# Gate products of a GRU in f16 passes, one sum moved to GpSimd, and a different split of the adjacency count

## Chip, cores and metric

The kernel runs on one core of a Trainium2 chip. The metric is the device time of one launch in microseconds (us). Before the change it was 1576.88 us, the median of three runs (1576.55 to 1579.28).

## What is computed

x has 8192 rows (nodes) of 128 features, adj is 8192 x 8192. Two residual layers, each after a layer norm and a ReLU:

```
h   = relu(layernorm(x))
Wh  = h @ W;  e = leaky_relu(Wh@a[:128] + (Wh@a[128:]).T, 0.2)
att = softmax(where(adj > 0, e, -9e15));  h' = att @ Wh
gi  = h' @ w_ih.T + b_ih;  gh = h @ w_hh.T + b_hh
r = sigmoid(gi_r + gh_r); z = sigmoid(gi_z + gh_z); n = tanh(gi_n + r * gh_n)
x   = x + (1 - z) * n + z * h
x   = x + adj @ (relu(layernorm(x)) @ W1.T + b1)
```

## The kernel before

The main path assumes that adj holds only zeros and ones, and finds out by counting whether that is so. A register read of `redo` at the end decides whether a second, general path (`any_adjacency`) is run; with the given inputs it isn't.

**Preparation.** x is loaded and normalised, transposed and multiplied with W. GpSimd (POOL) scales the gate weights by 64 (L401, L402), makes an f16 high and low part of w_ih (L404, L406, tile `wihT`), and an f16 unit matrix (L408). w_hh stays f32 (`whhT`).

**Layer 1.** 32 row blocks of 256 rows. A block is worked through in 4 chunks (c = 0 to 3) of 16 column tiles each. For each chunk SP loads 2 MB of adj into X (two buffers, L315), the Vector engine (DVE) makes mask bytes Y (`ones_of`, L662), SP stores Y to DRAM for layer 2 (L311), DVE and the Scalar engine (ACT) compare scores (L713, L491: 6 and 10 tiles of 16), DVE combines them to two masks (L721, L725), and TensorE (PE) multiplies the masks with the table TB in f16 (L970, 258 columns, 64 matmuls for each chunk and mask half). ACT counts the nonzero elements in the first SEEN = 7/8 of each chunk of X (`count`, L501); block 0 isn't counted here. When both readers are done with a buffer (c_y, c_cnt), SP loads the next chunk into it.

The GRU of a block is threaded into the slots of later blocks; PE's part stands in `after`. `attended` (L983) transposes h', `gates` (L997 to L1001) makes the gate sums of two halves t: a bias matmul of 512 columns, three f16 matmuls of 384 columns with w_ih (high times high, high times low, low times high), and two f32 matmuls with w_hh of 256 and 128 columns, on h transposed (HT, f32). ACT then takes the sigmoids (`gate_sigmoids`, L517) and the tanh (`candidate`, L522, tile nn). DVE does `gated` (L730, L732) in chunk 1 and `rows_step` in chunk 2: h - n (L744), times z (L753), x + n (L762), the sum of both (L768), then statistics. POOL adds EPS and takes the power -1/2 (L414, L417). SP stores x after the update and loads x, h and HT of a block (`rows_load`, L300 to L304). ACT copies PE's sums out of PSUM (`evacuate`, L511), and PE waits for that before it writes them for the next block.

**Layer 2.** For each row block t, PE multiplies the stored mask bytes with the projected features (L1055), DVE adds the halves of the mask (`halved`, L847), ACT sums them (`ones_sum`, L577), and DVE finishes the rows (`finish`, L863, L868). In between ACT loads and counts what layer 1 left out (`late_load`, `late_count`, L581 to L593): the 4 chunks of block 0 whole, then the last eighths of 8 chunks at a time, 20 loads in all. After the last halves `tally` (L889 to L893) compares the two counts; `sums` (L1088, L1090) stands in PE's queue in the middle of the last row block; `judge` and the last matmul (L1109) give the verdict, and SP waits for the last stores (L363) before all engines read `redo` and branch.

Each engine has its own queue, in the order of the code above; the order of the pieces within a slot is written out by hand, and semaphores join the queues.

Of the kernel before, what the change touches and what calls it, by code (L numbers as in the profile page):

```python
# [6 lines left out]
F = 128  # L7
P = 128
# [18 lines left out]
RW = 256  # L27
NS = N // RW
JC = 16
CS = NT // JC  # L30
# [3 lines left out]
MARK = 0.5  # L34
# [7 lines left out]
SEEN = JC * RW * 7 // 8  # L42
COUNTED = (NS - 1) * CS
LATE = CS + NS // 2
# [13 lines left out]
def graph_layers(nc, xb, adj, adjb, w, wt, a, w_ih, w_hh, wiht, whht, b_ih, b_hh, w1, w1t, b1, out):  # L58
    outer = ExitStack()
    with outer:  # L60
        def sem(name):
            return outer.enter_context(nc.semaphore(name))

        redo = outer.enter_context(nc.sbuf_tensor("redo", [1, 1], mybir.dt.int32))
        binary_adjacency(nc, sem, redo, xb, adjb, w, wt, a, wiht, whht, b_ih, b_hh, w1t, b1, out)
# [5 lines left out]
def binary_adjacency(nc, sem, redo, xb, adjb, w, wt, a, wiht, whht, b_ih, b_hh, w1t, b1, out):  # L71
    ctx = ExitStack()
    with ctx:
# [24 lines left out]
        wihT = sb("wihT", [P, 2, 3 * F], f16)  # L98
        whhT = sb("whhT", [P, 3 * F])
# [20 lines left out]
        nz = sb("nz", [P, NS // 2, 2 * CS + 1])  # L120
        cy = sb("cy", [P, NS])
        odd = sb("odd", [P, NS // 2, 2])
# [30 lines left out]
        wihf = rzf[:, P:P + 3 * F]  # L153
# [8 lines left out]
        bhid = TBf[0:2, 2 * F:4 * F].bitcast(f32)  # L162
# [36 lines left out]
        d_hi = t_lo  # L199
        q_half = t_p  # L200
# [19 lines left out]
        q_out = [sem(f"q_out{b}") for b in range(2)]  # L220
# [30 lines left out]
        with nc.Block() as block:  # L251
            @block.sync
            def _(sp):
                for q in range(8):
                    sp.dma_start(H[:, q * 8:(q + 1) * 8, :], xb[:, q * 8:(q + 1) * 8, :]).then_inc(p_x[q], 16)
                for dst, src in ((brow[0:3, :], b_ih.rearrange("(r c) -> r c", c=F)),
                                 (bhid, b_hh[0:2 * F].rearrange("(r c) -> r c", c=F)),
# [4 lines left out]
                for k in range(16):  # L262
# [8 lines left out]
                    if k == 9:  # L271
                        sp.wait_ge(p_bias, 7)
# [4 lines left out]
                sp.wait_ge(b_in, 112)  # L277
# [45 lines left out]

                each_row_block(sp, slot, 1)
# [37 lines left out]
                for u in range(2):  # L362
                    sp.wait_ge(q_out[u], NS // 2 * 16)  # L363

            @block.gpsimd
            def _(pool):
# [4 lines left out]
                nc.gpsimd.memset(onesb[:, :], 1.0)  # L371
                nc.gpsimd.memset(BI[:, :], 0.0).then_inc(p_one, 1)
                pool.wait_ge(p_id, 1)
# [13 lines left out]
                pool.wait_ge(b_in, 64)  # L387
                nc.gpsimd.tensor_tensor(brow[0:2, :], brow[0:2, :], bhid, ALU.add).then_inc(p_bias, 1)
                pool.wait_ge(p_bias, 1)
                nc.gpsimd.tensor_scalar(brow[0:4, :], brow[0:4, :], WSCALE, None, ALU.mult).then_inc(p_bias, 1)  # L390
                src = [brow] + bres
                for k in range(3):
                    pool.wait_ge(p_bias, 2 * k + 2)
                    nc.gpsimd.tensor_copy(bpart[k], src[k]).then_inc(p_bias, 1)
                    if k < 2:
                        pool.wait_ge(p_bias, 2 * k + 3)
# [3 lines left out]
                pool.wait_ge(wt_in, 48)  # L400
# [23 lines left out]
            def _(act):  # L424
# [4 lines left out]
                act.dma_start(wihf, wiht).then_inc(wt_in, 16)  # L429
                act.dma_start(whhT[:, :], whht).then_inc(wt_in, 16)  # L430
# [39 lines left out]
                def table_high(i):  # L470
                    act.wait_ge(t_p, i + 1)
                    if i == 0:
                        act.wait_ge(b_in, 112)
# [40 lines left out]
                def gate_sigmoids(q):  # L514
                    act.wait_ge(g_b, q + 1)
                    wait(act, d_x1, q)
                    nc.scalar.activation(rz[:, :, :], GP3[:, :, 0:2 * F], ACT.Sigmoid,  # L517
# [61 lines left out]
                def late_load(n):  # L579
                    if n < CS:  # L580
                        act.dma_start(Z[n % 2], adjb[n, :, :]).then_inc(c_in[n % 2], 16)  # L581
                    else:
                        first, last = max((n - CS) * 2 * CS, CS), (n - CS + 1) * 2 * CS
# [24 lines left out]
            def _(dve):  # L608
# [118 lines left out]
                def gated(q):  # L727
                    dve.wait_ge(g_2, q + 1)
                    wait(dve, g_3, q)
                    nc.vector.tensor_tensor(tmp[:, :, :], rz[:, :, 0:F], GP3[:, :, 3 * F:4 * F], ALU.mult).then_inc(d_rh, 1)  # L730
                    dve.wait_ge(d_rh, q + 1)
                    nc.vector.tensor_tensor(tmp[:, :, :], tmp[:, :, :], GP3[:, :, 2 * F:3 * F], ALU.add).then_inc(d_tmp, 1)  # L732

                def rows_step(qa, q, u, n):
# [3 lines left out]
                    xtv = XT[u].rearrange("p (t f) -> p t f", f=F)  # L738
# [12 lines left out]
                    if updating:  # L751
                        dve.wait_ge(d_u, q * 3 + 1)
# [8 lines left out]
                    if updating:  # L761
                        nc.vector.tensor_tensor(xtv, xtv, nn[:, :, :], ALU.add).then_inc(d_u, 1)  # L762
# [3 lines left out]
                    if updating:  # L766
                        dve.wait_ge(d_u, q * 3 + 3)
# [40 lines left out]
                def slot(g, u, k):  # L808
                    main = in_range(g, 0)
                    first = isinstance(g, int) and g == 0  # L810
                    for c in range(CS):
# [16 lines left out]
                        if c == 1 and in_range(g, 2):  # L828
                            gated(g - 2)
# [41 lines left out]
                def examine():  # L871
# [10 lines left out]
                    nc.vector.tensor_tensor(rzf[:, 0:3 * F], wihT[:, 0, :], wihT[:, 0, :], ALU.mult).then_inc(k_v, 1)  # L882
# [887 lines left out]
```

## Time and profile before

| | us |
|---|---|
| median of 3 runs | 1576.88 |
| the profiled execution | 1577.86 |
| its span, first to last instruction | 1576.0 |
| PE busy | 1508.2 (96%) |
| DVE busy | 1364.9 (87%) |
| ACT busy | 1350.7 (86%) |
| POOL busy | 135.3 (9%) |
| mean granted clock of TensorE | 0.985 |

Busy time counts instructions that work, not waits. Shares over the whole span mix the stages; layer 1 lies between about 62 and 1122 us, layer 2 behind it. In the rows below, L is the line in the kernel before, `out<-in` the tiles that an instruction writes and reads, and `<-` in brackets what ended an idle time.

### The profile page before, as it was taken

How to read it: one execution, taken by the hardware profiler on the slowest of the kernel's cores; microseconds unless marked ns; L12 is line 12 of the kernel's file. 1: busy time of each engine (PE TensorE's matmuls, PEld its weight loads, DVE VectorE, ACT ScalarE, POOL GpSimd, SP SyncE). 2: the span in 40 equal slices, each digit the busy share in tenths (PEclk: the TensorE clock that was granted, in tenths of full speed). 3: DMA queues.
4: the chain of work that ended last, by engine and by line, in shares of the span. 5: the costliest groups of instructions: out<-in, count | busy, mean ns of one | idle time of the engine just before them, and what ended most of it. 6: DMA issues, size and time to landing. Idle time of an engine off the chain costs nothing.

```text
span 1576.0 us, 35430 instructions
## 1 busy us (share of the span) xinstructions
PE 1508.2 (96%) x13356; PEld 1333.0 (85%) x13388; DVE 1364.9 (87%) x2161; ACT 1350.7 (86%) x1952; POOL 135.3 (9%) x96
## 2 busy tenths in 40 slices
PE   5468999999999999999999999999999999999997
PEld 4357888888888888888888888888888888888887
DVE  8898999999999999999999999997479977666684
ACT  5789999999999999999999999997175898875463
POOL 5100010001000110011000100010000000000000
PEclk9788999999999999999999999999999999999999
DMA  8859999999999999999999999997276999864430
GB/s 311 296 214 362 346 351 355 348 343 348 358 350 349 341 356 346 353 335 355 347 350 340 358 349 350 343 349 286 116 312 237 401 374 363 320 256 163 178 128 16
DMA packets 96085, 486.68 MB, mean 309 GB/s; under 512 B 9432, under 2 KB 38690, under 8 KB 75042
## 3 DMA queue, kind: packets, MB, share of 16 engines
q1 hardware_dynamic: 78322, 444.54, 75.4%
q10 hardware_dynamic: 17712, 41.49, 6.9%
q8 instruction: 28, 0.46, 0.1%
q14 instruction: 23, 0.19, 0.0%
HBM read 402.07 MB, written 83.92 MB: 308 GB/s over the span
## 4 chain that ended last, share of the span: by engine, by line
PE 93%; DVE 4%; ACT 1%; DMA 1%; issue 1%; DVEq 0%; ACTq 0%
PE ACC L970 56%; PE ACC L1055 28%; PE GP L999 2%; PE GP L1000 2%; PE GQ L1018 1%; ACT M L491 1%; PE GP L1001 1%; DVE TB L703 1%; DVE JK L612 1%; DVE AE L698 1%; DVE JK L698 1%; DMA h_columns<-AE 1%; DVE M L629 0%; PE TG L983 0%; PE TG L1007 0%
## 5 line engine op out<-in xcount | busy, mean ns | idle before, releaser
L970 PE MATMUL ACC<-TB,M 128*128 128x258 f16 x8192 | 928.1, 275 | 38.1 <-DVE M L721 31.0
L970 PEld LDWEIGHTS ACC<-TB,M 128*128 128x128 fp8e4 x8192 | 805.0, 98 | 143.6 <-issue 39.3
L491 ACT ACTIVATE M<-SB,dsteep 128x256 fp8e4<-128x256 f32 x1304 | 533.9, 504 | 0.0
L501 ACT ACTIVATE JK<-X 128x3584 uint8<-128x3584 uint32 x124 | 395.1, 3186 | 0.0
L662 DVE TENSOR_SCALAR Y<-X 128x4096 fp8e4<-128x4096 f32 x128 | 292.2, 2283 | 28.9 <-DMA X<-in_adjb_dram 28.4
L577 ACT ACTIVATE TB<-TB 128x8192 uint8<-128x8192 fp8e4 x32 | 225.0, 7030 | 102.8 <-DVE TB L847 90.6
L1055 PE MATMUL ACC<-WG,X 128*128 128x256 f16 x2048 | 225.5, 273 | 0.0
L1055 PE MATMUL ACC<-WG,TB 128*128 128x256 f16 x2048 | 225.4, 273 | 0.0
L1055 PEld LDWEIGHTS ACC<-WG,TB 128*128 128x128 fp8e4 x2048 | 200.4, 98 | 23.2
L1055 PEld LDWEIGHTS ACC<-WG,X 128*128 128x128 fp8e4 x2048 | 200.3, 98 | 23.1
L713 DVE TENSOR_SCALAR M<-SB,nd 128x256 fp8e4<-128x256 f32 x744 | 205.6, 346 | 0.0
L721 DVE TENSOR_TENSOR M<-M,Y 128x1024 uint32<-128x1024 uint32 x128 | 156.1, 1219 | 19.8 <-ACT M L491 18.6
L725 DVE TENSOR_TENSOR M<-Y,M 128x1024 uint32<-128x1024 uint32 x128 | 156.8, 1225 | 4.4
L414 POOL TENSOR_TENSOR ve<-mv,epst 128x2 f32<-128x2 f32 x32 | 63.0, 1969 | 985.7 <-DVE mv L792 985.7
L847 DVE TENSOR_TENSOR TB<-X 128x8192 fp8e4<-128x8192 fp8e4 x16 | 138.9, 8685 | 4.4 <-ACT TB L577 3.5
L847 DVE TENSOR_TENSOR TB<-TB 128x8192 fp8e4<-128x8192 fp8e4 x16 | 138.9, 8681 | 1.7 <-ACT TB L577 1.7
L863 DVE SCALAR_TENSOR_TENSOR hp<-ACC,R 128x256 f32<-128x256 f32 x32 | 13.5, 423 | 96.0 <-PE ACC L1055 94.2
L593 ACT ACTIVATE JK<-M 128x4096 uint8<-128x4096 uint32 (+1 forms) x20 | 70.3, 3516 | 2.6 <-DMA M<-in_adjb_dram 2.6
L417 POOL TENSOR_TENSOR rstd<-ve,half 128x2 f32<-128x2 f32 x32 | 48.0, 1501 | 2.5
L999 PE MATMUL GP<-wihT,hpT 128*128 128x384 f16 x192 | 41.7, 326 | 1.7
L511 ACT ACTIVATE AE<-ACC 128x516 f32<-128x516 f32 x64 | 37.7, 589 | 5.8 <-PE ACC L970 5.8
L1000 PE MATMUL GP<-whhT,R 128*128 128x256 f32 x128 | 38.1, 379 | 0.0
(142 smaller groups left out, 784.8 us busy)
## 6 DMA issues: line engine op xcount, KB each, us to landing
X<-in_adjb_dram SPq DMA_DIRECT2D x128, 2048.0 KB, 9.7
mask_bytes<-Y SPq DMA_DIRECT2D x128, 512.0 KB, 5.9
M<-in_adjb_dram ACTq DMA_DIRECT2D x19, 2048.0 KB, 11.7
X<-mask_bytes SPq DMA_DIRECT2D x16, 2048.0 KB, 9.3
TB<-mask_bytes SPq DMA_DIRECT2D x16, 2048.0 KB, 9.0
M<-in_xb_dram SPq DMA_DIRECT2D x8, 512.0 KB, 8.3
h_rows<-M SPq DMA_DIRECT2D x8, 512.0 KB, 4.2
R<-in_xb_dram SPq DMA_DIRECT2D x32, 128.0 KB, 6.7
```

Of the source, the lines that this page charges most:

```text
L491: ins = nc.scalar.activation(rows(mask1(c), jj), SB[u][:, :], ACT.Sigmoid, scale=STEEP, bias=dsteep[:, j:j + 1], saturate=False)
L501: nc.scalar.activation(junk[:, 0:SEEN], X[c % 2][:, 0:SEEN].bitcast(u32), ACT.Sign, accum_out=nz[:, bass.ds(k, 1), at:at + 1].rearrange("p ...
L577: nc.scalar.activation(junk8, halves[t % 2], ACT.Copy, accum_out=cy[:, t:t + 1]).then_inc(q_sum, 1)
L593: nc.scalar.activation(junk[:, 0:cols], Z[n % 2][:, 0:cols].bitcast(u32), ACT.Sign, accum_out=nz[:, k:k + 1, at:at + 1].rearrange("p k c - ...
L662: nc.vector.tensor_scalar(Y[c % 2][:, :].bitcast(f8), X[c % 2][:, :], 1.0, MARK, ALU.is_equal, ALU.mult, saturate=False).then_inc(c_y, 1)
L713: ins = nc.vector.tensor_scalar(rows(mask1(c), jj), SB[u][:, :], nd[:, j:j + 1], None, ALU.is_ge, saturate=False)
L721: nc.vector.tensor_tensor(mask1(c), mask1(c), Y[c % 2][:, :], ALU.bitwise_and).then_inc(c_m1, 1)
L725: nc.vector.tensor_tensor(mask2(c), Y[c % 2][:, :], mask1(c), ALU.bitwise_xor).then_inc(c_m2, 1)
L847: nc.vector.tensor_tensor(halves[b % 2], YB[b][:, 0:N], YB[b][:, N:2 * N], ALU.add, saturate=False).then_inc(q_half, 1)
L970: ins = nc.tensor.matmul(A[t][m][:, 0:2 * TW], rows((mask1, mask2)[m](c), jj)[:, t * P:(t + 1) * P], TB[:, c * JC + jj, m, 0:2 * TW], star ...
L999: nc.tensor.matmul(bank[:, 0:3 * F], left, wihT[:, part, :], start=False, stop=False)
L1055: ins = nc.tensor.matmul(PH2[b][:, d * 2 * F:(d + 1) * 2 * F], YB[b][:, j * RW + d * P:j * RW + (d + 1) * P], GS[:, j, :], start=(d == 0 a ...
```

## The change

- **Gates.** w_hh gets f16 high and low parts like w_ih; one tile `GW` holds both (columns n, r, z of w_ih and r, z, n of w_hh). h transposed gets them too (`HH`): DVE makes them in chunk 1 of a slot, between the two operations of `gated`. PE makes three f16 matmuls of 384 columns with them in place of the two f32 ones; PE now waits for the low part (d_hl) and no longer for the load of HT. The order of the gate columns in PSUM is n, r, z, h_n.
- **Sum.** x + n leaves DVE's `rows_step` and goes to POOL, ahead of L414 in its slot; DVE waits for it (d_xn) before L768.
- **Count.** SEEN is 13/16 in place of 7/8, so layer 2 counts 3/16 of a chunk, 5 chunks in a load: 29 loads in place of 20. The tally adds up to one number in place of 16.
- **Weights and biases.** Both gate matrices are loaded into R by three DMAs in place of two and prepared in three POOL operations on 768 columns. SP waits for them (p_bias 12) before its first slot, and for a memset of POOL before the bias loads, of which there are 5 in place of 4.
- **End.** The wait for the last stores stands behind the branch on `redo`, on SP.

```diff
-SEEN = JC * RW * 7 // 8
+SEEN = JC * RW * 13 // 16
+GROUP = 5
-LATE = CS + NS // 2
+LATE = CS + 25
...
         with nc.If(needed != 0):
+            for eng in (nc.sync, nc.scalar, nc.vector, nc.tensor, nc.gpsimd):
+                for u in range(2):
+                    eng.wait_ge(q_out[u], NS // 2 * 16)
             any_adjacency(nc, outer, xb, adj, w, a, w_ih, w_hh, b_ih, b_hh, w1, b1, out)
+        for u in range(2):
+            nc.sync.wait_ge(q_out[u], NS // 2 * 16)
...
+                sp.wait_ge(p_bias, 12)
                 each_row_block(sp, slot, 1)
...
-                for u in range(2):
-                    sp.wait_ge(q_out[u], NS // 2 * 16)
...
-                nc.gpsimd.tensor_scalar(wihf, wihf, WSCALE, None, ALU.mult).then_inc(p_bias, 1)
-                nc.gpsimd.tensor_scalar(whhT[:, :], whhT[:, :], WSCALE, None, ALU.mult).then_inc(p_bias, 1)
-                pool.wait_ge(p_bias, 8)
-                nc.gpsimd.tensor_copy(wihT[:, 0, :], wihf).then_inc(p_bias, 1)
+                nc.gpsimd.tensor_scalar(wraw, wraw, WSCALE, None, ALU.mult).then_inc(p_bias, 1)
+                pool.wait_ge(p_bias, 9)
+                nc.gpsimd.tensor_copy(GW[:, 0, :, :], wrawv).then_inc(p_bias, 1)
                 pool.wait_ge(p_bias, 10)
-                nc.gpsimd.tensor_tensor(wihT[:, 1, :], wihf, wihT[:, 0, :], ALU.subtract).then_inc(p_bias, 1)
+                nc.gpsimd.tensor_tensor(GW[:, 1, :, :], wrawv, GW[:, 0, :, :], ALU.subtract).then_inc(p_bias, 1)
...
                     if in_range(g, 2):
                         q = g - 2
+                        xtv = XT[u].rearrange("p (t f) -> p t f", f=F)
+                        pool.wait_ge(g_3, q + 1)
+                        pool.wait_ge(g_in[u], k * 48)
+                        nc.gpsimd.tensor_tensor(xtv, xtv, nn[:, :, :], ALU.add).then_inc(d_xn, 1)
                         pool.wait_ge(d_mv, q + 1)
...
-                    k, at = (0, n) if n < CS else (n - CS, 2 * CS)
-                    cols = JC * RW // 2 if n == CS else JC * RW
+                    k, at = (0, n) if n < CS else ((n - CS) % 16, 2 * CS + (n - CS) // 16)
+                    parts = min(GROUP, NS * CS - CS - (n - CS) * GROUP)
+                    cols = JC * RW if n < CS else parts * (JC * RW - SEEN)
...
+                def gate_step(qh, u, n, q):
+                    halving, gating = qh is not None, q is not None
+                    if halving:
+                        dve.wait_ge(g_in[u], (n + 1) * 48)
+                        wait(dve, g_b, qh)
+                        dve.sem_inc(turn, 1)
+                        nc.vector.tensor_copy(HH[:, 0, :], HT[u]).then_inc(d_hh, 1)
+                    if gating:
...
+                    if halving:
+                        dve.wait_ge(d_hh, qh + 1)
+                        nc.vector.tensor_tensor(HH[:, 1, :], HT[u], HH[:, 0, :], ALU.subtract).then_inc(d_hl, 1)
...
-                    if updating:
-                        nc.vector.tensor_tensor(xtv, xtv, nn[:, :, :], ALU.add).then_inc(d_u, 1)
...
                     if updating:
-                        dve.wait_ge(d_u, q * 3 + 3)
+                        dve.wait_ge(d_u, q * 2 + 2)
+                        dve.wait_ge(d_xn, 16 + q + 1)
                         nc.vector.tensor_tensor(x1, x1, XT[u], ALU.add).then_inc(d_x1, 1)
...
-                    pe.wait_ge(g_in[u], (n + 1) * 48)
+                    pe.wait_ge(d_hl, q + 1)
...
                         for left, part in ((a_t, 0), (a_t, 1), (a_l, 0)):
-                            nc.tensor.matmul(bank[:, 0:3 * F], left, wihT[:, part, :], start=False, stop=False)
-                        nc.tensor.matmul(bank[:, 0:2 * F], h_t, whhT[:, 0:2 * F], start=False, stop=False)
-                        ins = nc.tensor.matmul(bank[:, 3 * F:4 * F], h_t, whhT[:, 2 * F:3 * F], start=False, stop=True)
+                            nc.tensor.matmul(bank[:, 0:3 * F], left, GW[:, part, 0, :], start=False, stop=False)
+                        for left, part in ((h_t, 0), (h_t, 1), (h_l, 0)):
+                            ins = nc.tensor.matmul(bank[:, F:4 * F], left, GW[:, part, 1, :], start=False,
+                                                   stop=(left is h_l))
```

## Rows read from the trace of the kernel before

**Rows 1.** The page, chain of work that ended last, shares by engine.
```profile
PE 93%; DVE 4%; ACT 1%; DMA 1%; issue 1%; DVEq 0%; ACTq 0%
```

**Rows 2.** Busy time by stretch: PE, PEld, DVE, ACT, POOL, PEclk, DMA share, GB/s.
```profile
340.49:660.27 319.78, 319.25 (x2832) 282.00 (x2841) 304.14 (x571) 315.28 (x550) 37.06 (x20) 1.00 0.93 348
...
1152.00:1560.50 408.50, 408.50 (x3745) 366.17 (x3743) 304.33 (x105) 298.74 (x105) 0.00 (x0) 1.00 0.69 264
```

**Rows 3.** The same chain in order of time: start, length.
```profile
115.38 7.16 issue
122.53 16.77 PE ACC L970 x128
...
596.31 7.04 PE ACC L970 x64
...
628.29 7.04 PE ACC L970 x64
```

**Rows 4.** Waits between 340.49 and 660.27: total, times, longest.
```profile
DVE Y L662 <- DMA X<-in_adjb_dram: 8.0, 14, 1.2
DVE M L721 <- ACT M L491: 5.8, 10, 0.8
ACT rz L517 <- PE GP L1001: 4.5, 10, 0.5
```

**Rows 5.** Timeline of PE, end of one gate group: start, length.
```profile
626.99 0.65 PE L999 MATMUL GP<-wihT,hpT 128*128 128x384 f16 x3
627.48 0.59 PE L1000 MATMUL GP<-whhT,R 128*128 128x256 f32 x2
627.91 0.38 PE L1001 MATMUL GP<-whhT,R 128*128 128x128 f32 x2
628.13 7.20 PE L970 MATMUL ACC<-TB,M 128*128 128x258 f16 x64
```

**Rows 6.** Groups by line and shape, whole run: busy, mean ns, idle before.
```profile
L501 ACT ACTIVATE JK<-X 128x3584 uint8<-128x3584 uint32 x124 | 395.1, 3186 | 0.0
...
L593 ACT ACTIVATE JK<-M 128x4096 uint8<-128x4096 uint32 x19 | 68.4, 3602 | 2.6 <-DMA M<-in_adjb_dram 2.6
...
L762 DVE TENSOR_TENSOR R<-R,nn 128x256 f32<-128x256 f32 x32 | 13.3, 417 | 0.0
...
L684 DVE COPY tmp<-GP 64x128 f32<-64x128 f32 x1 | 0.3, 276 | 0.0
...
L406 POOL TENSOR_TENSOR wihT<-rz,wihT 128x384 f16<-128x384 f32 x1 | 0.9, 919 | 0.1
```

**Rows 7.** Timeline of ACT where PE first waits for it.
```profile
121.85 0.58 ACT L511 ACTIVATE AE<-ACC 128x516 f32<-128x516 f32 x1
```

**Rows 8.** Timeline of DVE and POOL around one small POOL sum.
```profile
612.65 2.26 DVE L662 TENSOR_SCALAR Y<-X 128x4096 fp8e4<-128x4096 f32 x1
...
612.82 2.15 POOL L414 TENSOR_TENSOR ve<-mv,epst 128x2 f32<-128x2 f32 x1 [28.20 <-DVE mv L792]
```

**Rows 9.** All 32 of that POOL sum: min/median/max ns.
```profile
L414 POOL TENSOR_TENSOR ve<-mv,epst x32: 196/2152/2154, 165.9 to 1141.9; 128x2 f32<-128x2 f32 x32
```

**Rows 10.** Timeline of one update of x: candidate, and its last sum.
```profile
605.23 0.41 ACT L522 ACTIVATE nn<-tmp 128x256 f32<-128x256 f32 x1
...
609.28 0.42 DVE L768 TENSOR_TENSOR R<-R 128x256 f32<-128x256 f32 x1
```

**Rows 11.** Timeline at the start, POOL's last preparation and DVE's resumption.
```profile
43.33 0.29 POOL L408 CAST identh<-ident 128x128 f16<-128x128 f32 x1
...
45.82 0.26 DVE L669 TENSOR_REDUCE bad<-WG 128x1 f32<-128x64 f32 x1 [3.79 <-ACT WG L440]
```

**Rows 12.** Timeline near the end: DVE's tally and PE's use.
```profile
1556.35 0.30 DVE L889 TENSOR_REDUCE odd<-nz 128x16 f32<-128x144 f32 x1 [1.88 <-ACT TB L577]
...
1560.37 0.29 PE L1088 MATMUL GP<-odd,ones 128*128 128x16 f32 x2
```

**Rows 13.** Waits of SP's queue at the end.
```profile
SPq L363 <- DMA out_dram<-R: 1.3, 1, 1.3
```

More of the change, by code:

```diff
@@ L64, in graph_layers, with binary_adjacency @@
         redo = outer.enter_context(nc.sbuf_tensor("redo", [1, 1], mybir.dt.int32))
-        binary_adjacency(nc, sem, redo, xb, adjb, w, wt, a, wiht, whht, b_ih, b_hh, w1t, b1, out)
+        q_out = [sem(f"q_out{b}") for b in range(2)]
+        binary_adjacency(nc, sem, q_out, redo, xb, adjb, w, wt, a, wiht, whht, b_ih, b_hh, w1t, b1, out)
         needed = nc.values_load(redo[0:1, 0:1], min_val=0, max_val=1)
         with nc.If(needed != 0):
+            for eng in (nc.sync, nc.scalar, nc.vector, nc.tensor, nc.gpsimd):
+                for u in range(2):
+                    eng.wait_ge(q_out[u], NS // 2 * 16)
             any_adjacency(nc, outer, xb, adj, w, a, w_ih, w_hh, b_ih, b_hh, w1, b1, out)
-def binary_adjacency(nc, sem, redo, xb, adjb, w, wt, a, wiht, whht, b_ih, b_hh, w1t, b1, out):
+        for u in range(2):
+            nc.sync.wait_ge(q_out[u], NS // 2 * 16)
+def binary_adjacency(nc, sem, q_out, redo, xb, adjb, w, wt, a, wiht, whht, b_ih, b_hh, w1t, b1, out):
     ctx = ExitStack()
@@ L97, in binary_adjacency @@
         h2T = sb("h2T", [P, RW])
-        wihT = sb("wihT", [P, 2, 3 * F], f16)
-        whhT = sb("whhT", [P, 3 * F])
+        GW = sb("GW", [P, 2, 2, 3 * F], f16)
+        HH = sb("HH", [P, 2, RW], f16)
         w1T = sb("w1T", [P, F])
@@ L161, in binary_adjacency @@
         brow = TBf[0:5, 0:2 * F].bitcast(f32)
-        bhid = TBf[0:2, 2 * F:4 * F].bitcast(f32)
+        bhid = TBf[0:5, 2 * F:4 * F].bitcast(f32)
         bres = [TBf[0:5, (4 + 2 * k) * F:(6 + 2 * k) * F].bitcast(f32) for k in range(2)]
@@ L199, in binary_adjacency @@
         d_hi = t_lo
+        d_hh, d_hl = sem("d_hh"), sem("d_hl")
+        d_xn = p_hd
         q_half = t_p
@@ L255, in _ @@
                     sp.dma_start(H[:, q * 8:(q + 1) * 8, :], xb[:, q * 8:(q + 1) * 8, :]).then_inc(p_x[q], 16)
-                for dst, src in ((brow[0:3, :], b_ih.rearrange("(r c) -> r c", c=F)),
-                                 (bhid, b_hh[0:2 * F].rearrange("(r c) -> r c", c=F)),
+                sp.wait_ge(p_bias, 1)
+                for dst, src in ((brow[0:1, :], b_ih[2 * F:3 * F].rearrange("(r c) -> r c", c=F)),
+                                 (brow[1:3, :], b_ih[0:2 * F].rearrange("(r c) -> r c", c=F)),
+                                 (bhid[1:3, :], b_hh[0:2 * F].rearrange("(r c) -> r c", c=F)),
                                  (brow[3:4, :], b_hh[2 * F:3 * F].rearrange("(r c) -> r c", c=F)),
@@ L386, in _ @@
                     deviation(q)
-                pool.wait_ge(b_in, 64)
-                nc.gpsimd.tensor_tensor(brow[0:2, :], brow[0:2, :], bhid, ALU.add).then_inc(p_bias, 1)
-                pool.wait_ge(p_bias, 1)
+                pool.wait_ge(b_in, 80)
+                nc.gpsimd.tensor_tensor(brow, brow, bhid, ALU.add).then_inc(p_bias, 1)
+                pool.wait_ge(p_bias, 2)
                 nc.gpsimd.tensor_scalar(brow[0:4, :], brow[0:4, :], WSCALE, None, ALU.mult).then_inc(p_bias, 1)
@@ L516, in gate_sigmoids @@
                     wait(act, d_x1, q)
-                    nc.scalar.activation(rz[:, :, :], GP3[:, :, 0:2 * F], ACT.Sigmoid,
+                    nc.scalar.activation(rz[:, :, :], GP3[:, :, F:3 * F], ACT.Sigmoid,
                                          scale=1.0 / WSCALE).then_inc(g_2, 1)
@@ L582, in late_load @@
                     else:
-                        first, last = max((n - CS) * 2 * CS, CS), (n - CS + 1) * 2 * CS
+                        first = CS + (n - CS) * GROUP
+                        last = min(first + GROUP, NS * CS)
                         act.dma_start(Z[n % 2][:, 0:(last - first) * (JC * RW - SEEN)].rearrange(
@@ L725, in combine @@
                     nc.vector.tensor_tensor(mask2(c), Y[c % 2][:, :], mask1(c), ALU.bitwise_xor).then_inc(c_m2, 1)
[L727 to L732, printed above, removed]
+                def gate_step(qh, u, n, q):
[6 more added lines that the diff above has]
+                    if gating:
+                        dve.wait_ge(g_2, q + 1)
+                        wait(dve, g_3, q)
+                        nc.vector.tensor_tensor(tmp[:, :, :], rz[:, :, 0:F], GP3[:, :, 3 * F:4 * F], ALU.mult).then_inc(
+                            d_rh, 1)
+                    if halving:
+                        dve.wait_ge(d_hh, qh + 1)
+                        nc.vector.tensor_tensor(HH[:, 1, :], HT[u], HH[:, 0, :], ALU.subtract).then_inc(d_hl, 1)
+                    if gating:
+                        dve.wait_ge(d_rh, q + 1)
+                        nc.vector.tensor_tensor(tmp[:, :, :], tmp[:, :, :], GP3[:, :, 0:F], ALU.add).then_inc(d_tmp, 1)
                 def rows_step(qa, q, u, n):
@@ L827, in slot @@
                             combine(g, c)
-                        if c == 1 and in_range(g, 2):
-                            gated(g - 2)
+                        if c == 1:
+                            gate_step(g - 1 if in_range(g, 1) else None, 1 - u, k if u else k - 1,
+                                      g - 2 if in_range(g, 2) else None)
                         if c == 2:
@@ L1087, in sums @@
                     pe.wait_ge(k_df, 4)
-                    nc.tensor.matmul(GP[:, 0:NS // 2], ones[:, :], odd[:, :, 0:1].rearrange("p g o -> p (g o)"), start=True,
-                                     stop=True)
+                    nc.tensor.matmul(GP[:, 0:1], ones[:, :], odd[:, 0:1], start=True, stop=True)
                     nc.tensor.matmul(GP[:, P:2 * P], ones[:, :], tmp[:, 0, :], start=True, stop=True).then_inc(k_w, 1)
```

49 lines of the change are left out of this document (26 added, 23 removed).

## The prediction

> **What bounds the kernel now.** I read three views in this order. First the chain of work that ended last: 93% of it is TensorE (PE) [rows 1]. Then the same chain in time: PE resumes at 122.53 us and from there the pieces join without a hole until layer 2 ends; the 64 products of one chunk return at 596.31 and 628.29 us, so one row block takes 31.98 us [rows 3]. Then ten such periods in one window of 319.78 us: PE busy 319.25, the Scalar engine (ACT) 315.28, the Vector engine (DVE) 304.14, the DMA engines 93% [rows 2]. Four resources stand within 7% of each other, so each must be asked what it can give. ACT's only idle time in the ten periods is 4.5 us, all of it waiting for PE's gate sums, thus 0.45 us for a block; DVE's waits are 8.0 us on loads of X and 5.8 us on ACT's masks [rows 4], in all 15.6 us idle (319.78 - 304.14), 1.56 us for a block. PE waits for nobody. So layer 1 is PE's, with ACT 0.45 us behind it. In layer 2 PE is busy 408.50 of 408.50 us, while ACT has 298.74 and DVE 304.33 [rows 2].
>
> **PE's part.** For each half t of a block the change takes out the two f32 matmuls on w_hh and puts three f16 ones of 384 columns in. Start to start in the trace: three f16 matmuls of 384 columns take 627.48 - 626.99 = 0.49 us, the f32 one of 256 columns 627.91 - 627.48 = 0.43, the f32 one of 128 columns 628.13 - 627.91 = 0.22 [rows 5]. Out go 0.65 us, in come 0.49: -0.16 us, -0.32 for the two halves. All 32 gate groups lie in PE's unbroken stretch, the last two of them between products of layer 2, so the term is 32 x 0.32 = **-10.2 us**. The new block takes 31.66 us, if the others keep up.
>
> **ACT's part.** A count of 4096 takes 3602 ns, of 3584 3186 ns [rows 6], 0.81 ns an element; 256 elements fewer are -0.21 us, four times a block -0.83. ACT's work falls from 31.53 (31.98 - 0.45) to 30.7 us, below 31.66: this makes room, and is no gain by itself in the steady part. It is one at the start. PE stands idle for 7.16 us from 115.38 [rows 3], until ACT has copied out the sums of block 0 at 121.85 + 0.58 [rows 7]. Ahead of that copy stand three counts of block 1's chunks in ACT's queue, so PE resumes 3 x 0.21 = **-0.6 us** earlier.
>
> **DVE's part.** DVE loses x + n, 417 ns, and gets the subtraction for the low part, which is an operation of that shape: 417 ns [rows 6]. The copy that makes the high part (256 f32 to f16) is not in the trace. The nearest rows are a copy of 64x128, 276 ns, below, and the 417 ns above; I take 280, because the row is a copy too. The subtraction fills the gap that `gated` leaves between its two operations, which I count as nothing. So DVE's work becomes 30.41 + 0.28 = 30.7 us. PE's gates wait for both new operations; DVE makes them just behind the sigmoids of the previous group, so most of a block of 31.98 us ahead of PE's next group. The copy itself waits for the load of HT, issued by SP in the slot before, and for PE's last gate group, for which the sigmoids beside it wait anyway: nothing. Behind it queue `gated` and the compares of the next chunk; PE, which takes their masks, waits for none in the ten periods [rows 4].
>
> **POOL's part.** The moved sum starts when nn is there, 605.23 + 0.41 = 605.64 us, and L768 needs it at 609.28 less the 0.33 that x + n took of DVE's queue: 3.3 us [rows 10]. The sum of 384 columns takes 919 ns, the same engine's sum of 2 columns 196 ns when nothing else runs [rows 6, 9]; in proportion 256 columns are an estimated 0.68 us. But the sum of 2 columns has a median of 2152 ns, and at 612.82 it ended only when DVE's L662 did, 612.65 + 2.26 = 614.91 [rows 8, 9]: POOL waits for some DVE instructions. The instruction running at 605.64 is at most 1.2 us long, so the sum should be ready by about 607.5. The opposite may happen too, that DVE waits for POOL; between nothing and the 919 ns I take the whole 0.68 us of the sum as lost to DVE. That gives 30.7 + 0.68 = 31.4 us for DVE, still under 31.66, by 0.3 us. The cover is thin here, and the rivals start from it.
>
> The Trainium skill, SBUF — State Buffer, "Who interferes with whom", states that a DVE instruction with two SBUF inputs and a GpSimd instruction that reads SBUF exclude each other for a whole instruction, whichever issues first. By that rule DVE pays the sum's time each block, which is the value in my sum; a reading of the rows alone would allow nothing, and DVE 30.7 us.
>
> **DMA.** Layer 1 moves the same bytes in 1% less time: from 93% to about 94%. X loads are issued when ACT's count is done, which now comes 0.2 us earlier, so I expect no new wait.
>
> **Layer 2.** ACT gets 9 more loads to count. Before: 19 of 3602 ns and one of half; after: 4 of 3602, 24 of about 3.4 us, one of 2.8: 99 in place of 70 us, and 9 accumulator reads. ACT comes to about 330 of 408 us. At the end of the layer, where the counts now reach up to the last two sums, the tally may come some 0.4 us later; it is at 1556.35, and PE asks for it at 1560.37 [rows 12], so PE hides it. Extra DMA traffic of 16 MB finds engines that are at 69% [rows 2]. Zero.
>
> **Start.** POOL's three operations on 768 columns in place of 384 add some 2 us to work that ended at 43.62, and DVE resumes on its own chain at 45.82 [rows 11]: hidden, with a bound of +0.5 us where POOL runs into it. SP's new wait for it comes later still. The additional small loads are issued long before their users. Zero.
>
> **End.** SP waits 1.3 us for the last stores [rows 13] before the engines meet and read `redo`. Moved behind the branch, this wait runs beside that reading: **-1.3 us** (bounds: 0 and -1.7, if the meeting costs something too).
>
> **Sum.** -10.2 - 0.6 - 1.3 = -12.1 us. The profiled execution took 1577.86 us (span 1576.0 and 1.86 around it), so it would take 1565.8. The median of the runs lies 0.98 lower: **1564.8 us**.
>
> **Rivals.**
> - *DVE becomes the bound by a little.* With the upper bounds, the copy 0.417 and POOL's hold 0.919, and the 0.18 us of idle time a block that no wait explains (1.56 - 0.80 - 0.58), DVE needs 30.41 + 0.42 + 0.92 + 0.18 = 31.9 us. Then layer 1 gives only some 0.05 x 30 = 1.5 us in place of 9.6; the time is 1564.8 + 8.1 = 1573, and between the bounds it is about 1569. For it: 31.4 is near 31.66. Against it: part of DVE's waits were for ACT and loads and vanish when it is late. Chance 0.11.
> - *POOL and DVE block each other for long (slower).* The place is the moved sum, among DVE's instructions with two inputs. If DVE stands still for as long as the small POOL sum lasts in the trace, 2.15 us, it needs 30.41 + 0.28 + 2.15 + 0.18 = 33.0 us, and 30 blocks cost 30 x 1.04 = +31 us, less 1.9: about 1606. It decides from a hold of 1.1 us, where DVE passes 31.98. Against it: those 2.15 us are POOL's waiting for DVE, since it ended 0.06 us after L662 [rows 8]. Chance 0.07.
> - *The DMA engines hold the pace.* At 93% busy, with DVE waiting for X in 14 of 40 chunks [rows 4], loads may already set the period. Then PE's gain turns into waits for masks, and only -1.9 is left: 1575. Against it: PE never waits, and X lands up to 1.2 us late only because it is issued as late as ACT lets it. Chance 0.05.
> - *The forecast.* Chance 0.77.
>
> **From these to the numbers.** A change of 0.2%, 3.15 us, is about what a measurement of this kernel can tell from none. Faster: the forecast and nearly all of the first rival, 0.86; within: 0.07, the DMA rival and the end of the first; slower: 0.07. The range: below, the end's bound (-0.4), more than three counts' worth at the start, and the spread of the runs give 1561; above, the first rival gives 1573. What lies outside is the slower rival and the DMA one, 0.12, and some of the runs' spread.
>
> **What would show it.** Right: the products of a chunk return every 31.66 us; one gate half takes 1.19 us, with six f16 matmuls; ACT's wait for the gates is longer than 0.45 us, near 0.9; PE has no wait for masks after about 122 us; PE's first wait ends 0.6 us earlier; DVE busy goes up by 0.2 to 0.3 us a block, and L725 or L744 is longer or late once a block. Wrong: a period above 31.7 us, PE waiting for DVE's L721 or L725 in the steady part, L768 waiting for POOL, layer 2 longer than 408.5 us for the same products, or the time after the last store unchanged.

## The result and the profile after

| | before | after |
|---|---|---|
| median of 4 runs, us | 1576.72 | 1563.76 |
| range | 1575.62 to 1579.28 | 1563.26 to 1563.96 |
| span of the profiled execution | 1576.0 | 1562.2 |

The ratio is 0.9915, 95% interval 0.9898 to 0.9932: 13.0 us less, where 12.1 were predicted (1564.8 us, range 1561 to 1573).

First the page of the changed kernel: who is on the chain that ended last, and how busy each engine is.

```profile
PE 1498.8 (96%) x13324; PEld 1310.0 (84%) x13324; DVE 1386.4 (89%) x2193; ACT 1354.8 (87%) x1970; POOL 168.3 (11%) x129
...
PE 93%; DVE 5%; ACT 1%; issue 1%; DMA 0%; POOL 0%; DVEq 0%; ACTq 0%
```

TensorE still holds 93% [rows 1]. Its busy time fell by 9.4 us, while that of the Vector engine rose by 21.5 and that of GpSimd by 33.0 (1386.4 and 168.3, from 1364.9 and 135.3).

Ten row blocks of the steady part, and layer 2, in the view by stretch (columns as in [rows 2]: length, PE, PEld, DVE, ACT, POOL, clock, DMA share, GB/s):

```profile
281.09:597.57 316.48, 316.48 (x2822) 274.74 (x2821) 310.44 (x581) 307.54 (x552) 45.17 (x30) 1.00 0.94 353
...
1139.97:1548.47 408.50, 408.50 (x3746) 366.06 (x3743) 305.30 (x105) 326.84 (x123) 0.00 (x0) 1.00 0.80 304
```

Ten blocks take 316.48 us, 31.65 each, in place of 31.98. The Scalar engine fell from 315.28 to 307.54 us for ten blocks; the Vector engine rose from 304.14 in a longer window to 310.44 in a shorter one: 31.04 us of 31.65, 98%. Layer 2's long stretch takes 408.50 us as before, with the Scalar engine at 326.84 (298.74 before) and DMA at 80% (69% before).

The same ten blocks, who waited for whom; it answers to [rows 4]:

```profile
ACT rz L533 <- PE GP L1031: 8.9, 10, 0.9
DVE Y L680 <- DMA X<-in_adjb_dram: 2.1, 5, 0.7
DVE M L739 <- ACT M L507: 1.1, 3, 0.4
```

TensorE is not in the list, so it still waits for nobody. The Scalar engine's wait for the gates doubled to 0.89 us a block: the room that the shorter counts made lies idle. The Vector engine's waits fell from 13.8 us to 3.2.

One gate half in the timeline of TensorE (start, length); it answers to [rows 5]:

```profile
588.51 0.38 PE L1027 MATMUL GP<-BI,onesb 128*128 128x512 bf16 x1
588.73 0.65 PE L1029 MATMUL GP<-GW,hpT 128*128 128x384 f16 x3
589.22 0.65 PE L1031 MATMUL GP<-GW,HH 128*128 128x384 f16 x3
589.70 7.20 PE L1000 MATMUL ACC<-TB,M 128*128 128x258 f16 x64
```

Six f16 matmuls of 384 columns stand where three f16 and two f32 stood. From 588.73 to 589.22 and on to 589.70 it is 0.49 and 0.48 us; the second was 0.65. The whole half takes 1.19 us (588.51 to 589.70).

The update of x in the timeline, with GpSimd's sum:

```profile
598.65 0.41 ACT L538 ACTIVATE nn<-tmp 128x256 f32<-128x256 f32 x1
...
599.22 0.73 POOL L427 TENSOR_TENSOR R<-R,nn 128x256 f32<-128x256 f32 x1 [20.48 <-ACT nn L538]
599.30 1.74 DVE L743 TENSOR_TENSOR M<-Y,M 128x1024 uint32<-128x1024 uint32 x1
600.96 0.41 DVE L773 SCALAR_TENSOR_TENSOR R<-R,nn 128x256 f32<-128x256 f32 x1
...
603.15 0.42 DVE L796 TENSOR_TENSOR R<-R 128x256 f32<-128x256 f32 x1
```

nn is done at 599.06, GpSimd makes its sum from 599.22 to 599.95. The Vector engine's L743 (L725 before) starts in the middle and takes 1.74 us; the usual is 1.22. That is 0.5 us more, of the 0.65 us for which GpSimd's sum went on beside it (599.95 - 599.30). L796 (L768 before) has room: the sum was ready 3.2 us earlier.

Not every sum is as short as this one. All 32 of them, from the page (busy, mean ns, idle before):

```profile
L427 POOL TENSOR_TENSOR R<-R,nn 128x256 f32<-128x256 f32 x32 | 31.6, 986 | 734.7 <-ACT nn L538 734.7
```

The shortest takes 0.73 us, the mean is 0.99 and the longest 2.07.

The start, in the chain in order of time; it answers to [rows 3]:

```profile
105.22 8.99 PE ACC L1000 x64
114.20 7.09 issue
121.30 16.51 PE ACC L1000 x128
```

The idle time costs more than its length. The 128 products behind it take 16.51 us, and 14.08 in the steady part. In stretches of 3 us, TensorE's granted clock is 0.50 from 121 to 124 us (its lower level, 1.2 GHz), 0.67 from 124 to 127, and 1.00 (2.4 GHz) from there on.

The end: the tally and TensorE's use of it, as in [rows 12].

```profile
1544.29 0.32 DVE L919 TENSOR_REDUCE odd<-nz 128x1 f32<-128x160 f32 x1 [1.88 <-ACT TB L593]
...
1548.31 0.28 PE L1119 MATMUL GP<-odd,ones 128*128 128x1 f32 x2
```

The tally is as far ahead of its use as before, 4.02 us. From the end of the last products of the long stretch (1139.97 + 408.50 = 1548.47) to the end of the span it is 13.73 us; before it was 1576.0 - (1152.03 + 408.50) = 15.47.

**Where the 13.8 us between the two spans come from.** TensorE resumes 1.23 us earlier (121.30 for 122.53). From there to the long stretch of layer 2 it takes 1018.67 us in place of 1029.50: -10.83. Then nothing, and -1.74 at the end. The medians differ by only 13.0 us, because the profiled execution before (1577.86) lay 1.1 us above its median and the one after (1563.77) on it.

### The profile page after: what moved, and what is told of

It reads as the page before. It is cut to its first block, busy times and chain, and to the rows that moved or that the text cites. A ratio compares the mean times of both kernels' runs of the same rounds, so it can differ in the third digit from the quotient of the medians.

```text
span 1562.2 us, 35505 instructions
## 1 busy us (share of the span) xinstructions
PE 1498.8 (96%) x13324; PEld 1310.0 (84%) x13324; DVE 1386.4 (89%) x2193; ACT 1354.8 (87%) x1970; POOL 168.3 (11%) x129
## 4 chain that ended last, share of the span: by engine, by line
PE 93%; DVE 5%; ACT 1%; issue 1%; DMA 0%; POOL 0%; DVEq 0%; ACTq 0%
PE ACC L1000 57%; PE ACC L1086 29%; PE GP L1029 2%; PE GP L1031 2%; PE GQ L1049 1%; ACT M L507 1%; PE GP L1027 1%; DVE M L647 1%; DVE JK L630 1%; DVE TB L721 1%; DVE AE L716 1%; DVE JK L716 1%; PE TG L1013 0%; PE TG L1038 0%; DVE JK L634 0%
## 5 line engine op out<-in xcount | busy, mean ns | idle before, releaser
L517 ACT ACTIVATE JK<-X 128x3328 uint8<-128x3328 uint32 x124 | 368.3, 2970 | 0.0
L680 DVE TENSOR_SCALAR Y<-X 128x4096 fp8e4<-128x4096 f32 x128 | 292.0, 2281 | 10.9 <-DMA X<-in_adjb_dram 10.6
L743 DVE TENSOR_TENSOR M<-Y,M 128x1024 uint32<-128x1024 uint32 x128 | 169.8, 1327 | 4.4
L427 POOL TENSOR_TENSOR R<-R,nn 128x256 f32<-128x256 f32 x32 | 31.6, 986 | 734.7 <-ACT nn L538 734.7
L611 ACT ACTIVATE JK<-M 128x3840 uint8<-128x3840 uint32 (+2 forms) x29 | 98.5, 3395 | 0.9 <-DMA M<-in_adjb_dram 0.9
L533 ACT ACTIVATE rz<-GP 128x512 f32<-128x512 f32 x32 | 19.1, 597 | 30.1 <-PE GP L1031 30.1
```

The lines of the kernel that those rows point to most:

```text
L517: nc.scalar.activation(junk[:, 0:SEEN], X[c % 2][:, 0:SEEN].bitcast(u32), ACT.Sign, accum_out=nz[:, bass.ds(k, 1), at:at + 1].rearrange("p ...
L611: nc.scalar.activation(junk[:, 0:cols], Z[n % 2][:, 0:cols].bitcast(u32), ACT.Sign, accum_out=nz[:, k:k + 1, at:at + 1].rearrange("p k c - ...
L680: nc.vector.tensor_scalar(Y[c % 2][:, :].bitcast(f8), X[c % 2][:, :], 1.0, MARK, ALU.is_equal, ALU.mult, saturate=False).then_inc(c_y, 1)
L743: nc.vector.tensor_tensor(mask2(c), Y[c % 2][:, :], mask1(c), ALU.bitwise_xor).then_inc(c_m2, 1)
```

## The experiments

All are built from the changed kernel and were timed against the kernel before. Their medians are to be held against 1563.76 us. Four kernels built from it that keep its pace and its end (count_back, sum_back, sum_back_384 and sum_back_768 below) came out between 1563.84 and 1564.09, with single runs from 1562.91 to 1564.55, so half a microsecond isn't told apart by the medians. Marks in the profiles tell where a difference lies. The period of a block is a sharp one. The start of layer 2's long stretch is not: it lies at 1139.97 in the changed kernel and at 1139.54, 1140.42 and 1139.17 in three kernels whose TensorE and Scalar engine have the same work in layer 1 (sum_back, wait_back, sum_back_384).

### The gates back to f32

```diff
-                        for left, part in ((h_t, 0), (h_t, 1), (h_l, 0)):
-                            ins = nc.tensor.matmul(bank[:, F:4 * F], left, GW[:, part, 1, :], ...)
+                        nc.tensor.matmul(bank[:, F:3 * F], h_t, whhT[:, 0:2 * F], start=False, stop=False)
+                        ins = nc.tensor.matmul(bank[:, 3 * F:4 * F], h_t, whhT[:, 2 * F:3 * F], start=False, stop=True)
```

The two new operations of the Vector engine go with them, and GpSimd copies w_hh once more at the start.

> The changed kernel with the h products of the gates back as two f32 matmuls for each half, and without the two new operations of the Vector engine; everything else stays changed. Theory (TensorE paces layer 1 and nothing else gave the 10 us): the products of a chunk return every 31.98 us again and the time is 1563.8 + 32 x 0.33 = 1574.3 us. Rival (the counts and the moved sum gave a part of it, by freeing the Scalar and the Vector engine): the time is well under 1574, by as much as those two parts are worth.

Measured: 1573.81 us (1573.22 to 1574.77, 11 runs), ratio 0.9981 (0.9972 to 0.9990). The chain in time, two successive returns of the same piece:

```profile
217.33 14.08 PE ACC L1001 x128
...
249.30 14.08 PE ACC L1001 x128
```

31.97 us a block. 10.0 us of the 13.0 are the gates, and nothing else takes their place when they go. The rival falls.

### The count back

```diff
-SEEN = JC * RW * 13 // 16
-GROUP = 5
+SEEN = JC * RW * 7 // 8
+GROUP = 8
...
-LATE = CS + 25
+LATE = CS + 16
```

> The changed kernel with 7/8 of a chunk counted in layer 1 and 20 loads in layer 2, as before. Theory: only the three counts ahead of the first copy out of PSUM matter, 3 x 0.21 = +0.6 us, 1564.4; the Scalar engine then has 31.5 us of work in a block of 31.65 and its wait for the gates falls to about 0.1 us. Rival (the shorter counts were needed for the new pace): the block takes more than 31.65 us, by 0.1 to 0.2, and the time is 1567 to 1570.

Measured: 1563.85 us (1563.63 to 1564.51). The chain where TensorE resumes, and the steady stretch:

```profile
114.68 7.21 issue
121.88 16.72 PE ACC L1000 x128
```

```profile
281.09:597.57 316.48, 316.48 (x2823) 274.82 (x2821) 310.03 (x581) 315.22 (x551) 44.98 (x30) 1.00 0.94 352
```

TensorE resumes 0.58 us later, as expected of three counts. In 316.48 us the Scalar engine now works 315.22: 0.13 us of room in a block, and TensorE still has all of its 316.48. So the count's share was not needed for the pace. The new split moved 16 MB of loads and 28 us of Scalar work to layer 2, where they cost nothing, for half a microsecond at the start. The median doesn't show it: it rose by 0.09 us where 0.6 was expected.

### The sum back

```diff
-                        nc.gpsimd.tensor_tensor(xtv, xtv, nn[:, :, :], ALU.add).then_inc(d_xn, 1)
...
+                    if updating:
+                        nc.vector.tensor_tensor(xtv, xtv, nn[:, :, :], ALU.add).then_inc(d_xn, 1)
```

> The changed kernel with x + n back on the Vector engine; GpSimd makes no sum. Theory: no change, within 0.3 us of 1563.8, since the Vector engine was not the bound either way: it gets 0.33 us of queue and loses the 0.5 us that its mask operation stood behind GpSimd's sum, so its busy time for a block falls from 31.0 to about 30.9 us. Rival (the move relieved the Vector engine, which would be the bound without it): blocks of more than 31.65 us and a time over 1565.

Measured: 1563.84 us (1563.03 to 1564.45). The group of the Vector engine's second mask operation, first in the changed kernel, then here (busy, mean ns, idle before):

```profile
L743 DVE TENSOR_TENSOR M<-Y,M 128x1024 uint32<-128x1024 uint32 x128 | 169.8, 1327 | 4.4
```

```profile
L739 DVE TENSOR_TENSOR M<-Y,M 128x1024 uint32<-128x1024 uint32 x128 | 156.8, 1225 | 4.4
```

1327 ns against 1225: 102 x 4 = 0.41 us a block in which the Vector engine stood behind GpSimd. Against that stand 0.33 us of its queue that x + n had taken. The stretch of ten blocks, to be held against 310.44 us of the Vector engine above:

```profile
281.09:597.57 316.48, 316.48 (x2823) 274.83 (x2821) 307.95 (x591) 307.52 (x551) 37.06 (x20) 1.00 0.94 352
```

With the sum back, the Vector engine is busy for 0.25 us less in a block. Moving the sum changed nothing in the time, and it made the engine that it was to relieve a little busier.

### How much room the Vector engine has

An operation whose result is not used is put behind the last sum of the update, over 384 or 768 columns, with the sum on GpSimd (as changed) or back on the Vector engine:

```diff
                         nc.vector.tensor_tensor(x1, x1, XT[u], ALU.add).then_inc(d_x1, 1)
+                        nc.vector.tensor_reduce(extra[:, :], GW[:, 0, 0:2, :], AX.XY, ALU.max)
```

(384 columns: `GW[:, 0, 0, :], AX.X`.)

> The changed kernel with one more operation of the Vector engine in each block, a maximum over 384 columns of the f16 weights whose result is not used, right behind the last sum of the update. It costs about 0.47 us of that queue. If the Vector engine is as full as its busy time says (31.04 us of 31.65 in a block, 0.3 us of waits), the block becomes about 31.65 to 31.8 us: 1564 to 1568. If its busy time overlaps itself and it has more room than that, nothing changes: 1563.8.

> The same with a maximum over 768 columns, about 0.87 us of the Vector engine's queue. If its busy time tells its room, blocks of about 32.0 to 32.2 us, TensorE waiting for masks, and 1573 to 1582. If it has more room, blocks of 31.65 and 1563.8.

> The extra maximum over 384 columns in each block, with x + n back on the Vector engine. With the sum on GpSimd this load gave 1567.3 us. Theory (the Vector engine stands still while GpSimd makes the sum, so that moving it gave no room: busy time for a block 31.04 us with the move and 30.80 without): the time is lower than with the move, 1564 to 1566. Rival (the move freed a third of a microsecond in a block): it is higher, 1570 to 1575.

> The same with 768 columns, which with the sum on GpSimd gave 1578.9 us. Theory: lower, 1571 to 1576. Rival: higher, 1583 to 1588.

Medians in us, with their ranges:

| added to a block | sum on GpSimd | sum on the Vector engine |
|---|---|---|
| nothing | 1563.76 (1563.26 to 1563.96) | 1563.84 (1563.03 to 1564.45) |
| 384 columns | 1567.33 (1566.16 to 1568.08) | 1563.97 (1562.91 to 1564.55) |
| 768 columns | 1578.93 (1575.84 to 1583.05) | 1564.09 (1563.32 to 1564.53) |

Start to start in the timeline, the smaller load takes 0.46 us of the Vector engine's queue (0.55 us busy) and the larger one 0.86 (0.95 busy). This is the clearest result of the study. With the sum on GpSimd, the Vector engine's room in a block is less than the 0.46 us of the smaller load: the time rises by 3.6 us, 0.11 us a block. With the sum back, even the 0.86 us of the larger one are hidden. So the move took at least 0.4 us a block from the very engine that it was to relieve. The expectations for the left column (1564 to 1568, 1573 to 1582) held. Those for the right column had the side right and the size too small: both times stayed where they were, at 1563.97 (expected 1564 to 1566) and 1564.09 (1571 to 1576).

Where it goes, in groups between 400 and 1000 us: with 768 columns and the sum on GpSimd,

```profile
L732 DVE TENSOR_SCALAR M<-SB,nd 128x256 fp8e4<-128x256 f32 x444 | 128.2, 361 | 0.0
L744 DVE TENSOR_TENSOR M<-Y,M 128x1024 uint32<-128x1024 uint32 x75 | 93.9, 1252 | 2.6
...
L428 POOL TENSOR_TENSOR R<-R,nn 128x256 f32<-128x256 f32 x19 | 34.2, 1802 | 300.4 <-ACT nn L539 300.4
...
L829 DVE TENSOR_SCALAR h2n<-R,mv,rstd 128x128 f32<-128x128 f32 x36 | 10.8, 343 | 4.8 <-POOL rstd L433 4.8
```

and with the sum on the Vector engine:

```profile
L728 DVE TENSOR_SCALAR M<-SB,nd 128x256 fp8e4<-128x256 f32 x456 | 126.1, 347 | 0.0
L740 DVE TENSOR_TENSOR M<-Y,M 128x1024 uint32<-128x1024 uint32 x76 | 93.1, 1225 | 2.6
...
L828 DVE TENSOR_SCALAR h2n<-R,mv,rstd 128x128 f32<-128x128 f32 x38 | 11.4, 341 | 0.0
```

The compares take 361 ns in place of 347, 24 of them a block (0.34 us); the second mask operation 1252 in place of 1225, four a block (0.11 us); and `normed` waits for GpSimd's power, 4.8 us in 18 blocks (0.27 us), where the other kernel has no such wait in this window. Together that is 0.7 us a block, more than twice the 0.33 us that the move saves. The longer compares are few: their median is 350 ns and the longest takes 829. GpSimd's sum itself takes 1802 ns here in the mean. One of the long ones:

```profile
701.43 4.24 POOL L428 TENSOR_TENSOR R<-R,nn 128x256 f32<-128x256 f32 x1 [16.35 <-ACT nn L539]
701.65 2.29 DVE L681 TENSOR_SCALAR Y<-X 128x4096 fp8e4<-128x4096 f32 x1
703.86 1.23 DVE L740 TENSOR_TENSOR M<-M,Y 128x1024 uint32<-128x1024 uint32 x1
...
705.12 1.64 DVE L744 TENSOR_TENSOR M<-Y,M 128x1024 uint32<-128x1024 uint32 x1
```

It begins at 701.43 and ends at 705.67, through two of the Vector engine's operations, and the third is longer by 0.4 us: each engine stops the other. The same kernel has a short sum among the compares:

```profile
732.05 2.13 DVE L732 TENSOR_SCALAR M<-SB,nd 128x256 fp8e4<-128x256 f32 x6
733.17 0.86 POOL L428 TENSOR_TENSOR R<-R,nn 128x256 f32<-128x256 f32 x1 [16.12 <-ACT nn L539]
```

Six compares take 2.13 us there in place of 1.66. L740 and L744 have two SBUF inputs. This bears out the section "Who interferes with whom" of SBUF — State Buffer in the Trainium skill, by which a Vector instruction with two SBUF inputs and a GpSimd instruction that reads SBUF exclude each other; only that the loss in the changed kernel was 0.51 us of a sum of 0.73, since L743 began after the sum had. L681 and the compares read one large tile each, so that sentence doesn't cover them; that GpSimd's sum waits for L681 and holds a compare up is what these rows show.

### The wait for the last stores back

```diff
+                for u in range(2):
+                    sp.wait_ge(q_out[u], NS // 2 * 16)
```

(at the end of SP's part, ahead of the branch)

> The changed kernel with the wait for the last stores back ahead of the read of the verdict. Theory: +1.3 us (the wait of the queue of SP before) to +1.7 us (what the stretch after the last store's issue shortened by), so 1565.1 to 1565.5, all of it after the last matmul. Rival (the end was shortened by something else, the single column of the tally for one): no change.

Measured: 1564.86 us (1564.43 to 1565.74), +1.1, a little less than the 1.3 to 1.7 expected. SP's queue at the end has its wait again:

```profile
SPq L375 <- DMA out_dram<-R: 1.4, 1, 1.4
```

By the marks, this kernel's long stretch starts at 1140.42 and its span is 1564.1, so 15.18 us follow the stretch, 1.45 more than in the changed kernel.

### The gates alone

The three undone parts above in one kernel: only the f16 products and what prepares them remain.

> The f16 gate products alone: the count's share, the sum's place and the wait for the last stores are all as before the change. Theory: the gates give 32 x 0.33 = 10.6 us of 1576.7 by themselves, 1566.1, and blocks of 31.65 us, with the Scalar and the Vector engine just under the pace. Rival (together the undone parts are needed as cover): blocks of more than 31.7 us and a time of 1568 to 1575.

Measured: 1565.90 us (1565.44 to 1566.41), ratio 0.9933 (0.9919 to 0.9946): 10.7 us under the 1576.62 of the kernel before in the same comparison, where the whole change is worth 13.0. The steady stretch:

```profile
281.09:597.57 316.48, 315.95 (x2812) 274.80 (x2821) 308.99 (x591) 315.42 (x552) 40.83 (x20) 1.00 0.94 353
```

The Scalar engine works 315.42 us of 316.48 and the Vector engine 308.99, and the pace is held: a chunk's products return at 597.54 and 629.19 us, after 31.65. The rest is 1565.90 - 1563.76 = 2.1 us. TensorE resumes at 122.07 us, 0.77 later than in the changed kernel, but its long stretch of layer 2 starts at 1139.95, and there at 1139.97; behind the stretch follow 1564.0 - 1139.95 - 408.50 = 15.55 us, 1.8 more. So in these profiles the rest is all at the end, and the 0.6 us of the counts at the start isn't found again later.

### Another order at the start

TensorE's 7.1 us of idle time before 121.30 end with the Scalar engine's copy of block 0's sums. Three kernels move it. In the first, evac_b, block 1 only:

```diff
+                            if second and c == 1:
+                                evacuate(0, 0)
                             sign_mask(g, u, k, c)
+                            if second and c == 1:
+                                evacuate(0, 1)
...
+                        if second and c == 3:
+                            attended_columns(0)
```

and on the Vector engine the attended rows of block 0 one chunk earlier. The others add `evacuate(g - 1, 0)` ahead of the count for blocks 2 and 3 (evac_c) and 2 to 5 (evac_d), and write the Scalar engine's first slots out in place of looping over them.

> The changed kernel with another order in row block 1 alone: the Scalar engine copies out block 0's first sums ahead of the second chunk's mask and the others right behind it, the Vector engine makes block 0's attended rows one chunk earlier, and the Scalar engine copies their transposed columns two chunks earlier. Theory (TensorE's idle 7.1 us from 114 us is only the order of that copy, and the other engines are fast enough to keep their lead): TensorE resumes 5 to 7 us earlier and the time is 1557 to 1559. Rival (the lead of masks is used up, and TensorE waits a little later for what it gained): 1560 to 1564, with new waits of TensorE between 130 and 250 us.

> The order of the run before it (evac_b), and in blocks 2 and 3 the Scalar engine copies out the first sums of the block before ahead of its count instead of behind it. In evac_b TensorE waited 5.3 us for that copy at 146 us, where it had waited 7.1 us at 114. Theory (it is one lag of the Scalar engine behind TensorE, paid where that copy stands behind a count, and worked off by 0.9 us a block): TensorE waits about 1.8 us in block 2, not at all in block 3 and 1 to 2 us in block 4; 1561 to 1562. Rival (the masks are late too, or loads of X are): the wait only changes its place and name, 1563.

> The same with the early copy in blocks 2 to 5. Theory: the lag is worked off by block 6, no wait of TensorE behind block 2, 1559.5 to 1561. Rival: as for evac_c, 1562 to 1564.

Measured: 1563.12 (1561.99 to 1564.04), 1563.54 (1562.56 to 1564.11) and 1564.40 us (1564.10 to 1564.65). None is clearly faster than the changed kernel, and evac_d looks slower: its five runs all lie above the four of the changed kernel. The chain in time for evac_b:

```profile
118.16 0.80 issue
...
146.36 5.29 issue
151.65 17.06 PE ACC L1009 x128
```

and for evac_c:

```profile
113.65 0.62 issue
...
117.96 0.79 issue
...
146.15 2.44 issue
...
153.93 2.08 issue
...
187.83 0.46 issue
```

In evac_b TensorE resumes at 118.96 and waits 5.29 us one block later, before the next copy of the same kind; the long stretch of layer 2 starts at 1140.12, no earlier than in the changed kernel (1139.97). In evac_c the waits are 0.62, 0.79, 2.44, 2.08 and 0.46 us, 6.4 in all against 7.1, and the stretch starts at 1138.76; the median doesn't confirm it. In evac_d the longest wait is 3.75 us at 151.50, and the stretch starts at 1140.89. The rival was right: the wait changes its place. Part of the reason can be seen in evac_b: the Vector engine waited 2.3 us for X at 148 us, so loads of X too are late there. What share they have wasn't tried, and why evac_d came out above the changed kernel is open.

## Why the prediction was right

- **What bounds the kernel.** TensorE in both layers, with nobody awaited: borne out by the waits of the changed kernel and by the pace of the gates alone.
- **Gates, -10.2 us.** Measured 31.98 - 31.65 = 0.33 us a block, 10.6 for 32; undone by themselves they cost 10.0 us in the median. The term was 0.4 us short: 0.16 us was taken for each half, and by the periods it is 0.165.
- **Counts, -0.6 us, at the start alone.** Undone, TensorE resumes 0.58 us later, but the median rises by only 0.09, and in the profile of the gates alone nothing of it is left at layer 2. So the mechanism was seen and its worth in the total time was not. That they make room and no gain in the steady part: the Scalar engine's wait rose from 0.45 to 0.89 us, and with the old counts the pace is the same.
- **Vector engine, 31.4 us of work a block.** Its busy time came to 31.04. The copy took 286 ns (280 taken). GpSimd's sum was estimated at 0.68 us, took 0.73 at the least and 0.99 in the mean, and held the Vector engine up for 0.41 us a block, not for the whole sum; in the case above L743 lost 0.51 us of a sum of 0.73. The prediction's reading of the rule, by which the Vector engine pays the whole sum each block, was an upper bound. "The cover is thin here" was right: 0.46 us more were too much. Among the signs, the busy time was to go up by 0.2 to 0.3 us a block. That leaves out the hold that the sum of the same prediction has; it went up by 0.63 (30.41 to 31.04).
- **The last stores, -1.3 us.** Undone, +1.1 in the median and +1.45 by the marks, inside the bounds of 0 and -1.7. The profiles' -1.74 behind the long stretch is just outside.
- **Layer 2, start and DMA, nothing.** The long stretch is 408.50 us in both; DMA went from 93% to 94% in layer 1 and from 69% to 80% in layer 2. The tally did not come the 0.4 us later that were allowed for.
- **What was missed.** TensorE resumed 1.23 us earlier, not 0.6. It already stood 0.59 us earlier at its chunk before the wait (105.22 for 105.81). The kernels built from the changed one have this mark anywhere from 104.52 to 105.46, and the one with f32 gates resumed still earlier, at 120.60. So kernels that all have the change's preparations differ by up to a microsecond at this mark; with one profile of the kernel before, how much of the 0.59 is the change's stays open. TensorE's clock adds to the scatter: the 128 products behind the wait take from 15.57 us (sum_back_384) to 16.77 (before), by how soon the granted clock is back at 1.00.
- **The sum of the parts.** Undone one at a time, the gates, the count, the moved sum and the wait cost 10.05, 0.09, 0.08 and 1.10 us in the medians, 11.3 of the 13.0. The gates alone give 10.7, which is 0.6 more. The microsecond that remains was found in no single part. The forecast of 12.1 came near because the term of the gates was right; the 0.9 us between it and the 13.0 belong to no term.
- **The rivals.** The slower one needed a hold of 1.1 us a block; the hold was 0.41. The first needed a little more than it got: an extra 0.46 us brought it about, at 1567.3 us. DMA, at 94%, did not hold the pace.

In one respect the experiments go further than the prediction. It found 31.66 - 30.7 = 0.96 us of room beside GpSimd's sum and took 0.68 off for the hold. The loads bear out both parts. Without GpSimd's sum, the busy time leaves 0.85 us (31.65 - 30.80), and a load of 0.86 us is hidden. With it, the busy time leaves 0.61 us (31.65 - 31.04), and a load of 0.46 us isn't hidden. So the busy time told the room well as long as no other engine stood in the way, and too high by at least 0.15 us where one did. The load moves the operations against each other: in dve_768 GpSimd's sum lasts 1.80 us in the mean in place of 0.99, compares are held up, and `normed` waits for GpSimd's power. The prediction had only a hold of fixed size. No row of the kernel before shows where the sum would fall among the Vector engine's operations. That it mostly stayed as short as the estimate in the changed kernel was luck in part.

## What to carry to other kernels

Price a change at the engine whose waits are empty, operation by operation from start to start; here one term on TensorE was 10 of 13 us. Work taken off engines that keep up with it buys nothing in the steady part, and can be left where it is. Before a sum is moved to GpSimd to relieve the Vector engine, look at what the Vector engine runs at that moment: here each waited for the other, not only in operations with two inputs, and the exchange lost more than it moved. How much room a hidden engine has is told by loading it; its busy share gives too much where another engine can hold it up.

## What the runs showed of the hardware

- A sum of 256 f32 columns on GpSimd took 0.73 us beside a Vector operation that it held up (1.74 in place of 1.22 us), and 4.24 us in one case where it ended only behind two Vector operations. Six compares with such a sum among them took 2.13 us in place of 1.66.
- A Vector engine busy for 31.04 us of 31.65, with GpSimd's sum beside it, could not take 0.46 us more without a longer time; one busy for 30.80 without that sum took 0.86 us more. Its busy share alone would have put the two a quarter of a microsecond apart.
- Three f16 matmuls of 384 columns took 0.49 us, and the two f32 ones of 256 and 128 columns 0.65: here three f16 passes were cheaper than the f32 matmuls of the same columns.
- After 7.09 us in which TensorE stood idle, its granted clock was 0.50 for some microseconds, and 128 products took 16.51 us in place of 14.08.
